# Shared blocks 1 to 3 of a gated mixture layer: row tiles turned by VectorE in 32x32 squares instead of by TensorE

## What is computed

```python
x = x + tanh(g_xattn) * xattn(layernorm(x), ids, ctx, ctx, ctx)   # Wg = Wu = Wd = ctx_2048
x = x + tanh(g_ffn) * ffn(layernorm(x), ...)

def xattn(h, ids, Wg, Wu, Wd):            # expert = min(ids // 6250, 3)
    y = (silu(h @ Wg[e].T) * (h @ Wu[e].T)) @ Wd[e].T

def ffn(x, gate_w, gate_b, W1, W3, W2, Ws1, Ws3, Ws2):
    scores = sqrt(softplus(x @ gate_w.T))
    _, idx = top_k(scores + gate_b, 2)    # of 16, capacity 256 each
    w = scores at idx, divided by their sum
    y = sum over the two of w * ((silu(x @ W1[e].T) * (x @ W3[e].T)) @ W2[e].T)
    return y + (silu(x @ Ws1.T) * (x @ Ws3.T)) @ Ws2.T
```

## Time and profile before

| | us |
|---|---|
| median of 3 runs | 473.88 |
| lowest, highest | 473.39, 474.53 |
| the profiled execution | 473.53 |
| its span in the trace | 471.6 |
| mean granted clock of TensorE in it | 0.998 |

### The profile page before, as it was taken

One profiled execution on the slowest core, in us unless ns is written; L12 is line 12 of the kernel. 1 busy time (PEld: TensorE's weight loads), 2 busy tenths in 40 slices (PEclk: granted clock), 3 DMA queues, 4 the chain that ended last, 5 costly groups with the idle time before them and its releaser, 6 DMA issues.

```text
span 471.6 us, 7815 instructions
## 1 busy us (share of the span) xinstructions
PE 456.1 (97%) x2487; PEld 391.7 (83%) x2487; DVE 320.3 (68%) x720; ACT 267.5 (57%) x415; POOL 212.0 (45%) x176
## 2 busy tenths in 40 slices
PE   2999999999999999999999999999999999999995
PEld 1577888888888888888888999999999999999994
DVE  6688988978876654479469676676656765576442
ACT  4656666666654643633345666656555666656441
POOL 0704445654443475426168344444525545442443
PEclk9999999999999999999999999999999999999999
DMA  8524876887654552254289998889869988888465
GB/s 298 178 105 125 267 242 204 280 279 253 229 201 158 171 158 96 46 68 62 35 224 166 300 310 256 263 282 275 255 207 260 258 274 257 256 272 245 51 126 94
DMA packets 30477, 95.29 MB, mean 202 GB/s; under 512 B 4976, under 2 KB 7024, under 8 KB 29936
## 3 DMA queue, kind: packets, MB, share of 16 engines
q0 software_dynamic: 17056, 43.92, 37.7%
q1 hardware_dynamic: 13104, 50.98, 31.4%
q10 hardware_dynamic: 288, 0.01, 0.0%
HBM read 67.77 MB, written 28.70 MB: 205 GB/s over the span
## 4 chain that ended last, share of the span: by engine, by line
PE 91%; DVE 4%; ACT 2%; issue 1%; DMA 1%; POOL 0%; POOLq 0%; ACTq 0%; DVEq 0%
PE psG L1435 48%; PE psY L1435 30%; PE psT L1440 7%; PE psG L1697 1%; PE psG L1464 1%; DMA tok_i<-in_ids 1%; PE psY L1452 1%; DVE stats L1013 1%; DVE xh_sb L1030 0%; DVE nwt L995 0%; DVE arena L1186 0%; DVE arena L1046 0%; POOL out L571 0%; PE psY L1741 0%; PE psY L1603 0%
## 5 line engine op out<-in xcount | busy, mean ns | idle before, releaser
L1435 PE MATMUL psY<-arena 128*128 (+1 forms) x366 | 89.2, 394 | 0.6 <-DVE arena L1042 0.6
L1435 PEld LDWEIGHTS psY<-arena 128*128 128x128 f32 x366 | 67.7, 188 | 14.9 <-issue 1.0
L530 POOL DMA_INDIRECT ht<-out,idx x32 | 33.7, 1053 | 66.6 <-PE psT L1440 50.8
L1435 PE MATMUL psY<-slot,arena 128*128 128x512 f32 x240 | 59.0, 395 | 0.0
L1179 DVE TENSOR_TENSOR slot<-raw,slot 128x1536 fp32r<-128x1536 f32 x25 | 43.9, 1757 | 21.0 <-ACT slot L683 20.9
L1435 PE MATMUL psG<-arena 128*128 x216 | 54.0, 398 | 0.0
L1179 DVE TENSOR_TENSOR arena<-raw,arena 128x1536 fp32r<-128x1536 f32 x24 | 42.0, 1757 | 17.4 <-ACT arena L683 17.4
L1435 PEld LDWEIGHTS psY<-slot,arena 128*128 128x128 f32 x240 | 44.3, 188 | 9.3 <-ACT xh_sb L727 0.3
L1435 PE MATMUL psG<-arena,slot 128*128 128x512 f32 x216 | 51.3, 392 | 0.0
L1435 PEld LDWEIGHTS psG<-arena,slot 128*128 128x128 f32 x216 | 40.1, 188 | 8.2
L1435 PEld LDWEIGHTS psG<-arena 128*128 128x128 f32 x216 | 39.2, 188 | 7.6
(11 more groups left out here) (250 smaller groups left out, 818.3 us busy)
## 6 DMA issues: line engine op xcount, KB each, us to landing
raw<-in_w SPq DMA_DIRECT2D x48, 768.0 KB, 5.5
padded<-xh_sb SPq DMA_DIRECT2D x19, 256.0 KB, 2.0
raw<-in_w SPq DMA_DIRECT2D x12, 192.0 KB, 3.3
raw<-in_ctx_t SPq DMA_DIRECT2D x2, 1024.0 KB, 8.8
ht<-in_ctx_t SPq DMA_DIRECT2D x1, 1024.0 KB, 11.8
xh_sb<-in_ctx_t SPq DMA_DIRECT2D x1, 1024.0 KB, 7.5
out<-log_sb SPq DMA_DIRECT2D x4, 256.0 KB, 3.0
ht<-out,idx POOLq DMA_INDIRECT x33, 4.3
```

What stands on the lines that cost most here:

```text
L530: pool.indirect_dma_start(ht[:, n, :], None, halves_of_out, slots(e * NA + a, 0)).then_inc(g_here[n], 16)
L1435: ins = pe.matmul(ps, left[a], right[b], start=n == 0 and m == 0, stop=n == total - 1 and m == 2)
```

## The change

For blocks 1 to 3 PE no longer transposes. POOL scatters each tile's norm once more, by rank, to `by_rank` (rows that pad a tile are dropped), so a row tile is 128 rows on end there, and SP loads it. For block 0 that is one load, and PE transposes as before, now with every fourth column together. For blocks 1 to 3 SP loads each tile in four quarters of 128 columns, each to 32 partitions, with the four groups of 32 tokens side by side; DVE then turns 32x32 squares (`turn`), straight into the bank that ACT and DVE read. The feature that stands on a partition is now another one (partition p holds features 4p to 4p + 3), so the shared weights are laid out to match, on the host.

The chunks come in another order, (0, 1) ahead of (2, 2), and DVE's and ACT's lists between the first stage and chunk 6 are written out anew. The logits' transposes take only the 16 rows that hold logits.

In the diff `load_rows` and the loop after it are SP's; the second scatter and `rank_rows` (five small operations, which make the indices `rank_of`) are POOL's, where `rank_gather` is gone; the wait on `ranked_sent` is that of DVE's residual, `turn` and the lists after it are DVE's; `transpose4_strided` and the rest, up to `SEQ`, are PE's.

```diff
+C_END = C_RANK + NT
+by_rank = nc.dram_tensor("by_rank", (TOK, D), F32).ap()
...
+        def quarters(ap):
+            return ap.rearrange("p (b i k) -> p k b i", b=KD, k=KD)
...
+            def load_rows(j):
+                all_landed(sp, ranked_sent, j + E1 - 1)
+                if j // TB == 2:
+                    sp.wait_ge(h_ready, 4 if j % TB < 2 else NT)
+                    sp.wait_ge(bT_ps, j - 7)
+                elif j >= TB:
+                    sp.wait_ge(bT_ps, j - 3 if j < 2 * TB else j - 7)
+                rows = by_rank[j * P:(j + 1) * P, :]
+                if j < TB:
+                    sp.dma_start(row_tile(j), rows).then_inc(ht_here[j % 8], 16)
+                else:
+                    for q in range(KD):
+                        sp.dma_start(row_tile(j)[q * QP:(q + 1) * QP, :].rearrange("t (b d) -> t b d", b=KD),
+                                     rows[:, q * P:(q + 1) * P].rearrange("(b t) d -> t b d", b=KD)).then_inc(ht_here[j % 8], 16)
             for t in range(NT):
                 sp.wait_ge(xh_ready, t + 1)
-                sp.dma_start(padded[t * P:(t + 1) * P, :], xh_sb[:, t % 2, D:2 * D]).then_inc(padded_sent[t % 2], 16)
...
+                if 6 <= t < 6 + TB:
+                    load_rows(t - 6)
+                elif t >= 11 and t - 7 < 3 * TB - 1:
+                    load_rows(t - 7)
+            for j in range(3 * TB - 1, NJ):
+                load_rows(j)
...
+                if t == 0:
+                    pool.wait_ge(rows_idx, 1)
+                pool.indirect_dma_start(by_rank, bass.IndirectOffsetOnAxis(ap=rank_of[:, t:t + 1], axis=0),
+                                        xh_sb[:, t % 2, D:2 * D], None,
+                                        bounds_check=TOK - 1, oob_is_err=False).then_inc(ranked_sent[t % 2], 16)
...
+            def rank_rows():
+                pool.wait_ge(r1_idx, 2)
+                pool.tensor_scalar(rank_f[:, 0, :], S(28, 2)[:, 0:NT], float(TOK), 2.0 * TOK,
+                                   ALU.is_ge, ALU.mult).then_inc(rank_steps, 1)
...
+                pool.tensor_copy(rank_of[:, :], rank_f[:, 3, :]).then_inc(rows_idx, 1)
...
+            rank_rows()
...
-                if SPLIT <= t < SPLIT + TB:
-                    rank_gather(t - SPLIT)
...
-                        dve.wait_ge(padded_sent[par], landed(t - 4, par))
+                        dve.wait_ge(ranked_sent[par], landed(t - 4, par))
...
+            def turn(j):
+                before = 0 if j < 8 else 16 if j - 8 < TB else 16 * KD
+                dve.wait_ge(ht_here[j % 8], before + 16 * KD)
+                dve.wait_ge(bT_ps, j)
+                if j >= TB + 2:
+                    dve.wait_ge(bT_lo, j - 1)
+                dve.transpose(row_bank(j), quarters(row_tile(j))).then_inc(bT_ps, 1)
...
+                if known == NT - 1:
+                    dve.wait_ge(hT_lo, NT)
+                    turn(TB)
                 if known == NT:
                     gate(0)
+                    dve.wait_ge(gT_lo, NT)
+                    turn(TB + 1)
...
                     if known == NT + 1:
                         transposed(TB)
                         transposed(TB + 1)
+                        turn(TB + 2)
+                        turn(TB + 3)
+                        transposed(TB + 2)
+                        transposed(TB + 3)
+                        low(0)
...
+            def transpose4_strided(ps, src):
+                for k in range(KD):
+                    ins = pe.transpose(ps[:, k * P:(k + 1) * P], src.rearrange("p (i k) -> p k i", k=KD)[:, k], ident)
+                return ins
...
-                    t = pe.transpose(psY[1][:, s], log_sb[:, s], ident)
+                    r = slice(LOG0, LOG0 + E2)
+                    t = pe.transpose(psY[1][:, j * P + LOG0:j * P + LOG0 + E2], log_sb[r, s], ident[r, r])
...
-            for n in range(1, NB):
-                transposed(n * TB)
-                transposed(n * TB + 1)
+            for n in range(1, 6):
                 half_up(n, 0)
                 if SEQ[n - 1][1] == 2:
                     logits_of(SEQ[n - 1][0])
-                transposed(n * TB + 2)
-                transposed(n * TB + 3)
                 half_up(n, 1)
...
-SEQ = [(0, 2), (0, 0), (1, 2), (2, 2), (3, 2), (0, 1)] + [(b, c) for b in range(1, NB) for c in range(2)]
+SEQ = [(0, 2), (0, 0), (1, 2), (0, 1), (2, 2), (3, 2)] + [(b, c) for b in range(1, NB) for c in range(2)]
...
+    for w in (w1, w3):
+        w[0] = w[0].transpose(1, 0, 2).reshape(P, KD, IP)
```

More of the change, by code:

```diff
@@ L34 @@
 KD = D // P
+QP = P // KD
 NJ = TOK // P
@@ L158, in gated_layer @@
         idx1 = sb("idx1", [P, NT, 2], I32)
-        idxc = sb("idxc", [P, 3, NJ], I32)
+        idxc = sb("idxc", [P, 2, NJ], I32)
+        rank_of = sb("rank_of", [P, NT], I32)
+        rank_f = sb("rank_f", [P, 4, NT])
         tile_e = sb("tile_e", [P, NT], I32)
@@ L244, in gated_layer @@
         r2_whot, r2_wsrc, r2_w = (sem(f"r2_{n}") for n in ("whot", "wsrc", "w"))
-        rank_hot, rank_src, rank_idx, rows_idx = (sem(n) for n in ("rank_hot", "rank_src", "rank_idx", "rows_idx"))
-        padded_sent = [sem(f"padded_sent{n}") for n in range(2)]
+        rank_hot, rank_src, rank_idx, rows_idx, rank_steps = (
+            sem(n) for n in ("rank_hot", "rank_src", "rank_idx", "rows_idx", "rank_steps"))
+        ranked_sent = [sem(f"ranked_sent{n}") for n in range(2)]
         xa_here = [sem(f"xa_here{n}") for n in range(4)]
@@ L276, in gated_layer, with S @@
         block = stack.enter_context(nc.Block())
+        def S(n, w=1):
+            return small[:, n * NJ:(n + w) * NJ]
         def as_f32(ap):
@@ L502, in _ @@
                 scatter(t - 2)
-                if SPLIT <= t < SPLIT + TB:
-                    rank_gather(t - SPLIT)
-                if ROWS0 < t <= ROWS0 + 2 * TB - 1:
-                    rank_gather(t - ROWS0 + TB - 1)
-            rank_gather(3 * TB - 1)
-            for j in range(3 * TB, NJ):
-                rank_gather(j)
             for b in range(NB):
@@ L733, in _ @@
             stage1(act, step)
-            for n in range(1, 5):
-                if 1 < n < NB:
-                    transposed(n * TB)
-                    transposed(n * TB + 1)
+            for n in range(1, 6):
+                if n < 4:
+                    transposed(2 * TB + 2 * n - 2)
+                elif n == 4:
+                    transposed(NJ - 1)
                 silu(n)
@@ L740, in _ @@
                     copy_logits(n)
-                if n < NB:
-                    transposed(n * TB + 2)
-                    transposed(n * TB + 3)
+                if n < 4:
+                    transposed(2 * TB + 2 * n - 1)
                 high(n)
-            split(0, 2, 0)
-            hidden(5)
+                if n == 3:
+                    transposed(NJ - 2)
+                elif n == 4:
+                    split(0, 2, 0)
             silu(6)
@@ L1221, in _ @@
             stage1(dve, step)
-            for n in range(1, 5):
-                if 1 < n < NB:
-                    transposed(n * TB)
-                    transposed(n * TB + 1)
-                if SEQ[n - 1][1] == 2:
-                    take_logits(SEQ[n - 1][0])
-                if n < NB:
-                    transposed(n * TB + 2)
-                    transposed(n * TB + 3)
-                gate(n)
-                low(n)
+            take_logits(0)
+            turn(8)
+            turn(9)
+            gate(1)
+            transposed(8)
+            low(1)
+            turn(10)
+            transposed(9)
+            turn(11)
+            transposed(10)
+            gate(2)
+            turn(12)
+            low(2)
+            transposed(11)
+            turn(13)
+            take_logits(1)
+            transposed(12)
+            turn(14)
+            gate(3)
+            transposed(13)
+            low(3)
+            turn(15)
+            transposed(14)
+            transposed(15)
+            gate(4)
+            low(4)
+            take_logits(2)
             split(0, 2, 0)
+            gate(5)
+            low(5)
             take_logits(3)
-            hidden(5)
             B = [x_[:, :, :] for x_ in big]
@@ L1613, in _ @@
                     logits_of(SEQ[n - 1][0])
-                transposed(n * TB + 2)
-                transposed(n * TB + 3)
                 half_up(n, 1)
-            half_up(4, 0)
-            logits_of(2)
-            half_up(4, 1)
-            half_up(5, 0)
             logits_of(3)
-            half_up(5, 1)
             up(6)
```

55 lines of the change are left out of this document (15 added, 40 removed).

## The result

| | before | with the change |
|---|---|---|
| median of four runs, us | 474.2 | 479.9 |
| lowest, highest, us | 473.39, 474.58 | 479.04, 481.05 |
| the profiled execution, us | 473.53 | 479.79 |
| its span in the trace, us | 471.6 | 477.8 |

The ratio of the two is 1.0114, with a 95% interval of 1.0099 to 1.0129: the medians differ by 5.7 us where 2.5 us more were forecast (476.0 us), and the time lies above the range. The span grew by 6.2 us.

What follows compares the result with a forecast made beforehand. The logits' way to the router was taken to hold PE's fourth down group; slow turns on DVE delay the last logit scatter from 190.19 to 192.7, so 473.53 + 2.5 = 476.0 us, range 471.8 to 478.0.

Steps and rivals of the forecast that it cites:

- What bounds the kernel: At PE's fourth down group: PE gains only what the logits gain, since that wait, 0.3 us, all but binds.
- the rival of the full saving: The whole 5.2 us of transposes taken off PE would arrive, 468.3 us; chance 0.01.
- The price of a turn: A DVE turn of 512 elements takes 1.06 us: 0.68 plus 0.37 for reading in steps of 16 bytes.
- Rival 1: DVE turns pay nothing for their stepped read: 0.69 us each, 472.3 us in all, or 471.0 at 0.49; chance 0.40.
- DVE late, and the sixth chunk at 179.5: DVE's queue from 151.9 us with ten turns ends at 179.3, so block 3's chunk starts at 179.5, not PE's own 174.5.
- its turn is due at 176.9. Covered by 3 us: SP's loads of rows 11 to 15: the last lands by 170.7 to 173.6, before DVE's turn, so costs nothing.
- Rival 2: SP's quarter loads land late: row 15 at 179.3 instead of 176.9, another 2.4 us, 478.4 us; chance 0.11.
- Eight scatters back to back, 7 x 1.26 = 8.8 us: POOL's logit scatters for blocks 2 and 3, at 1.26 us pitch; the last starts at 192.7 us.
- The end moves by the same: After the fourth down group PE has no gap, so the kernel's end moves by the same +2.5 us.
- the signs that the prediction named: Turns' mean, DVE without idle 152 to 179, PE's waits (1.8, 1.8, 3 us), last logit scatter at about 192.7.
- Costed at nothing: Scatter by rank, POOL's three extra transfers (3.8 us), block 0's strided transposes (at most 1.5 us) and the last tile's later norm.
- the worst that the prediction allowed for: The residual reusing the buffer of the scatter by rank would be 0.6 us late, only in its own tile.

Runs made afterwards that it cites:

- the moved low half: The change with DVE's low half of the third weight piece placed behind the copy of block 3's logits: 481.15 us, ratio 1.0167.
- the list edits on the change: The change with ACT's second row copy, the router's small matmul and the eighth chunk's gate and low part moved earlier in their lists: 475.12 us, 1.0028.

## Why the prediction was wrong

- **What bounds the kernel, and the rival of the full saving: right.** PE could gain only what the logits gain, and the order of the chunks rules the saving out. The order alone, tried on the kernel before, costs what the whole change costs.
- **The price of a turn: right.** 1.06 us were taken from line 1284, 1.10 measured. The share of the step, 0.73 ns per element, came out to the second digit, though line 1284 steps 64 bytes and a turn 16. The Trainium skill, page "Advanced Engine Details and Errata", section "SBUF Cachelines", says that each access to another 16-byte line is penalized; the two kernels agree, 0.37 us for 512 elements. Its page "Vector Engine (DVE) Microarchitecture Reference", section "The reshape front-end and per-opcode configuration", speaks of one element per cycle and lane for the 32x32 transpose; the 0.72 us of a turn in steps of one agree with that as far as the other one-pass operations do (0.68 us).
- **Rival 1, full rate: its condition can be made true, its time was wrong.** With turns of 0.72 us the kernel took 476.9 us, not 472.3. Row 12's quarters then held DVE 1.95 us, the long scatter stayed, and so did the hole.
- **DVE late, and the sixth chunk at 179.5: right, but for the quarters.** It started at 180.64; in two kernels with the same turns and loads whose profiled executions have no wait for the quarters (the moved low half, the list edits on the change) it started at 179.60 and 179.61. In the change DVE was without idle time from 154 to 179 but for 1.09 us ahead of row 12. The step that failed is "its turn is due at 176.9. Covered by 3 us": I looked at the last of the five rows. Row 12, the second in SP's queue, was due at 169.7, and its quarters landed at 170.8. A quarter took 0.43 us to issue instead of 0.32, and these landed after 5.11 us in the chain of waits. Rival 2 had the mechanism, for the wrong row.
- **Eight scatters back to back, 7 x 1.26 = 8.8 us: mis-sized by 0.8 us.** The first one met DVE's operation with two inputs in SBUF. With the quarters' 1.1 us the last scatter was 2.0 us behind the forecast (194.72 against 192.7), and the fourth down group 1.6 (202.60 against 198.49 + 2.5 = 201.0), since 0.3 us of slack were to be had.
- **"The end moves by the same": this step failed.** I foresaw TensorE waiting about 3 us ahead of the fourth down group and took a wait to cost its length. Behind that wait the clock was at 0.50, and nine matmuls took 1.8 us longer, about 0.3 of it the start behind a wait (2.33 against 2.07 at full clock) and the rest the clock; filling the hole with idle work gave 2.1 us back in the median. None of the signs that the prediction named looked at the clock. This is the largest single term of the miss: 1.8 of 6.2 - 2.5 = 3.7 us; the later start makes 1.6, and what comes behind 244 us 0.3.
- **Costed at nothing: right in the main.** Block 0's strided transposes on PE load their weights in 205 ns instead of 138, but four of them take 0.47 us in the chain of waits instead of 0.44, 0.1 us in all. One residual waited for the scatter by rank, 0.59 us ahead of 53.09, the worst that the prediction allowed for; TensorE was then 0.1 us behind the kernel before (the next tile's first product starts at 59.41 against 59.34), so it cost next to nothing. The logits' transposes on 16 columns, taken as no gain, went from 0.44 to 0.36 us, 0.3 us in all on an engine that waits later.

## What to carry to other kernels

Work taken off the busiest engine shows up only where no chain of fixed length (here copy, scatters, load, router step, row copy: 22.0 us from one chunk to one down group) sets the next meeting point; measure that chain, and try the reordering that comes with a change by itself. Price an idle hole of TensorE of two microseconds or more as its length plus, where the clock falls, the slower matmuls behind it (1.8 to 2.9 us in the kernels above that wait ahead of the fourth down group), and look first for a list in which the waiting instruction stands needlessly behind something else. Where a read with a step feeds the bottleneck, the neighbouring stepped operation of the same trace gives its price per element.

## What the runs showed of the hardware

- The clock does not follow the length of a hole alone. In the profiled executions it fell with holes of 1.97, 2.04, 2.93, 3.48, 3.55 and 3.65 us and with all longer ones (3.77 to 8.66), and not with holes of 2.08, 3.54 and 3.56 us in other kernels (six matmuls in 1.66 us, nine in 2.34 and 2.34). What decides between these is not shown here.
- An indirect transfer of POOL that begins while DVE runs an operation with both inputs in SBUF ends about 0.85 us behind that operation: about 1.75 us instead of 0.97 in the change and in each kernel that keeps the pair as the change has it, and so also where the operation was moved. It was there in the kernel before, in the timelines of POOL and DVE:

```profile
168.84 1.42 POOL L485 DMA_INDIRECT logit_rows<-ranked_logits,idxc  x1 [0.30 <-issue]
...
168.74 0.69 DVE L1202 TENSOR_TENSOR arena<-gu,arena 128x512 fp32r<-128x512 f32 x1 [0.70 <-ACT arena L714]
```

  The transfer ends at 170.26, 0.83 us behind the end of the low part at 169.43. Where the transfer begins first, neither is longer (188.35 and 188.47 in the change). The Trainium skill, page "SBUF — State Buffer", section "Who interferes with whom", says that such an operation contends with a GpSimd instruction that reads SBUF, through shared ports that are locked exclusively. The rows with DVE first fit that; those with POOL first show no wait of DVE. The same section infers that such an operation does not stall DMAs that GpSimd makes; for these transfers the rows differ, and they decide.
